# Two transformer-like layers on one core: write vectors shifted by DRAM rows, maxima turned on VectorE, work of the first layer moved between engines, and a new order

## The reference

```python
# first layer, attention place: a selective scan, then a perceptron, then a norm over (tokens, channels)
xm, res = split(xn @ in_proj_w.T);  xm = silu(causal_conv4(xm) + conv_b)
dt, B, C = split(xm @ x_proj_w.T);  delta = softplus(dt @ dt_proj_w.T + dt_proj_b)
h_t = exp(delta_t * A) * h_{t-1} + delta_t * B_t * u_t      # 512 channels x 16 states
y = (h_t . C_t + u * D) * silu(res);  m = y @ out_proj_w.T
c = m + gelu(m @ ffn_w1.T + ffn_b1) @ ffn_w2.T + ffn_b2
x = x + (c - mean(c)) / sqrt(var(c) + eps)                  # sequence 0's experts are in x too: gelu(x @ w1) @ w2, weighed
# second layer: causal softmax attention of 16 heads with 16 channels, and a memory
w1 = x_prev @ w1_write;  w2 = x @ w2_write                  # x_prev is x moved by one token, zero at token 0
write_lines = exterior(w1, w2);  read_lines = exterior(r1, r2)
mem_score = sum_j (read_i . J write_j)**2 * decay**(i - j)
out = x + (seq_out + mean(sigmoid(mem_score * s) * gate) * mem_val) @ out_w + out_b + perceptron(x)
```

## Time and profile before

| | |
|---|---|
| median of 3 runs | 3749.46 us (3745.34 to 3749.89) |
| the profiled execution | 3745.62 us, its span 3743.9 us |
| TensorE busy | 3543.0 us (95%) |
| VectorE busy | 3169.1 us (85%) |
| ScalarE busy | 2654.0 us (71%) |
| GpSimd busy | 2278.8 us (61%) |
| mean granted TensorE clock | 0.986 |

### The profile page before, as it was taken

How to read it: one execution, slowest core, us unless ns; L and a number is a source line. 1 busy time by engine, 2 the same in 40 slices (tenths; PEclk the granted TensorE clock), 3 DMA queues, 4 the chain that set the end, 5 groups by cost and what they waited for, 6 DMA issues and landing times.

```text
span 3743.9 us, 63558 instructions
## 1 busy us (share of the span) xinstructions
PE 3543.0 (95%) x20512; PEld 2364.9 (63%) x20512; DVE 3169.1 (85%) x6019; ACT 2654.0 (71%) x4087; POOL 2278.8 (61%) x1790
## 2 busy tenths in 40 slices
PE   7999999999999999999888999999999999999998
PEld 3666666656556665656665766767676676767665
DVE  3798999999999999999977688786968778696873
ACT  5878878788787878888634757566675757667565
POOL 3797999999999999999934142332514233251421
PEclk9999999999999999999898999999999999999999
DMA  4445445554554555545532123232312323231220
GB/s 155 134 162 166 161 148 181 155 170 163 167 167 148 177 166 166 170 149 178 191 97 97 42 78 101 70 109 70 115 48 81 98 70 115 64 122 48 75 84 21
DMA packets 253340, 456.88 MB, mean 122 GB/s; under 512 B 26116, under 2 KB 80852, under 8 KB 250196
## 3 DMA queue, kind: packets, MB, share of 16 engines
q1 hardware_dynamic: 253012, 452.82, 38.7%
HBM read 381.07 MB, written 69.21 MB: 120 GB/s over the span
## 4 chain that ended last, share of the span: by engine, by line
PE 50%; DVE 22%; issue 10%; ACT 8%; POOL 7%; DMA 2%; DVEq 0%; SPq 0%; POOLq 0%; ACTq 0%
DVE ps L2071 8%; PE ps L1661 6%; PE ps L1548 5%; PE ps L1653 5%; PE ps L1529 4%; POOL drive L2326 4%; PE ps L1511 3%; DVE heavy L2049 3%; ACT ps L1678 3%; PE ps L1413 3%; DVE held L2071 3%; PE ps L1463 2%; PE ps L1380 2%; ACT L1678 2%; PE ps L1588 2%
## 5 line engine op out<-in xcount | busy, mean ns | idle before, releaser
L2326 POOL TENSOR_TENSOR drive<-du,b_wide 128x1024 f32<-128x1024 f32 x512 | 1202.6, 2366 | 147.7 <-DVE held L2071 80.1
L1678 ACT ACTIVATE ps<-delta,neg_a 128x512 f32<-128x512 f32 x1024 | 684.4, 686 | 184.4 <-DVE heavy L2049 115.7
L1678 ACT ACTIVATE exps<-ps 128x1024 f32<-128x1024 f32 (+1 forms) x640 | 599.7, 939 | 228.9 <-PE ps L1529 224.9
L2360 POOL TENSOR_SCALAR_AFFINE_SELECT exps<-exps 128x256 f32<-128x256 f32 x512 | 204.4, 414 | 832.5 <-ACT exps L1678 832.5
L2094 DVE CUSTOM_DVE_ANT_0 ps<-ps,later 128x512 f32<-128x512 f32 (+3 forms) x1024 | 474.6, 518 | 55.1 <-PE ps L1511 53.1
L2049 DVE TENSOR_TENSOR heavy<-c_wide,ps 128x512 f32<-128x512 f32 x704 | 450.5, 676 | 15.2 <-issue 14.1
L1463 PEld LDWEIGHTS ps<-p_all,heavy 128*128 128x128 f32 x3072 | 355.2, 142 | 152.5 <-issue 76.9
L2071 DVE TENSOR_TENSOR_SCAN ps<-ps,carry,drive 128x512 f32<-128x512 f32 x352 | 434.8, 1274 | 10.6 <-ACT ps L1678 10.6
L1463 PE MATMUL ps<-p_all,heavy 128*128 128x128 f32 x3072 | 415.0, 277 | 23.3 <-DVE heavy L2049 20.8
L2071 DVE TENSOR_TENSOR_SCAN ps<-ps,drive 128x512 f32<-128x512 f32 x352 | 414.0, 1215 | 25.3 <-ACT ps L1678 21.9
L2310 POOL TENSOR_TENSOR held<-held,c_wide 128x1024 f32<-128x1024 f32 x160 | 378.4, 2365 | 6.4
(11 more groups left out here) (212 smaller groups left out, 7175.2 us busy)
## 6 DMA issues: line engine op xcount, KB each, us to landing
b_wide<-bc_dram SPq DMA_DIRECT2D x512, 256.0 KB, 3.4
c_wide<-bc_dram SPq DMA_DIRECT2D x512, 256.0 KB, 3.6
stacks<-parts SPq DMA_DIRECT2D x192, 256.0 KB, 2.5
qs<-stacks SPq DMA_DIRECT2D x128, 192.0 KB
ks<-stacks SPq DMA_DIRECT2D x128, 192.0 KB, 4.4
x_row<-in_x SPq DMA_DIRECT2D x14, 1024.0 KB, 7.9
resid<-mix SPq DMA_DIRECT2D x9, 1024.0 KB, 5.5
x_row<-resid SPq DMA_DIRECT2D x9, 1024.0 KB, 6.1
```

The lines of the kernel that those rows point to most:

```text
L1678: return nc.scalar.activation(out_, in_, func, **kw)
L2326: G.tensor_tensor(drive[:, g % DRIVE_SLOTS, :, :], du[:, e, :, :], wide(b_wide[:, g % B_SLOTS, :], MD), ALU.mult).then_inc(driven, 1)
```

## The change

It does the following.

- Prelude: 16 matmuls of the identity by itself before the first unit; the last four taps after the first norm, neg_a after xm; a Silu for each block of xm; Softplus on one column after the last; res units 0 and 1 moved into the order behind; the second du behind the first drive; a unit bias that transposes fb2 to late_bias.
- First layer: ScalarE drains o with a plain copy; fb2 is added in the drain of m instead, and fix (16 one-column matmuls and one subtraction) takes its product with the up weights out of fb1. gate_pair is one instruction. offset goes to GpSimd, square and shift to ScalarE.
- Second layer, memory: pb is one group of 320 columns; ScalarE drains the write vectors to ahead, and for each half SP stores them to DRAM rows one further (put) and loads them into pt1 (shift). The two memsets of a first column are gone.
- Second layer, maxima: the unit mt leaves TensorE; VectorE turns smax by four 32x32 transpositions (flip) to turned, from which mt works on ScalarE and VectorE.
- New lengths and SHIFTS for the planner, so all five lists have another order.

The diff, cut to its core:

```diff
-            + [("res", 0, t) for t in range(2)] + [("xd", 0)] + [("dl", 0, m) for m in range(MI)])
+            + [("xd", 0)] + [("dl", 0, m) for m in range(MI)] + [("bias", 0)])
...
+WARM = 16
...
                 dense(("pa", b, t), ("v", "xt", b, t // TC, KD - 1), ("v", "weights_lo", 1), ("p", "o", b - 1, NQ - 1, TQ - 1) if b else None,
                       ("v", "gate", b - 1, NC - 1) if b else None, ("p", "zt", b - 2, NC - 1, KD - 1) if b > 1 else None,
-                      a=[("g", "outer", (n - TC) // NT, (n - TC) % NT)] if n >= TC else [])
-                dense(("pb", b, t), ("p", "pa", b, t))
-                add("g", ("outer", b, t), 1.05, place["pb", b, t], ("a", "pb", b, t),
+                      a=([("g", "outer", (n - TC) // NT, (n - TC) % NT)] if n >= TC else []))
+                dense(("pb", b, t), ("p", "pa", b, t), a=[("s", "put", b - 1, NC - 1)] if b else [])
+                if t % TC == TC - 1:
+                    add("s", ("put", b, c), 0.45, place["pb", b, t], ("a", "pb", b, t), late=2.5)
+                    add("s", ("shift", b, c), 0.5, place["pb", b, t] + 1, ("s", "put", b, c),
+                        ("g", "outer", (n - TC) // NT, (n - TC) % NT) if n >= TC else None, late=2.9)
+            for t in range(TC * c, TC * (c + 1)):
+                n = NT * b + t
...
+                elif kind == "put":
+                    c = task[2]
+                    drained(sp, plan, ("pb", n, TC * c + TC - 1), "a")
+                    if (n, c) == (0, 0):
+                        sp.wait_ge(ahead_set, 1)
+                        sp.dma_start(ahead_rows[:, 0, :], none_ahead[0:B, :]).then_inc(ahead_put, 16)
+                    sp.dma_start(ahead_rows[n, 1 + c * HALF:1 + (c + 1) * HALF, :].rearrange("(t p) d -> p t d", p=P),
+                                 ahead[:, TC * c:TC * (c + 1), :]).then_inc(ahead_put, 16)
+                elif kind == "shift":
+                    c = task[2]
+                    sp.wait_ge(ahead_put, 16 * (NC * n + c + 2))
+                    if NC * n + c:
+                        sp.wait_ge(outer_done, TC * (NC * n + c))
+                    sp.dma_start(pt1[:, :, 0:64], ahead_rows[n, c * HALF:(c + 1) * HALF, :].rearrange("(t p) d -> p t d", p=P))\
+                      .then_inc(shifted, 16)
...
-                    pe.wait_ge(xm_silu, j + 1)
                     w = weight("xproj", MI)
+                    if j:
+                        pe.wait_ge(xm_silu, silus(j))
                     for m in range(MI):
+                        if j == 0:
+                            pe.wait_ge(xm_silu, m + 1)
                         last = mm(bank[0:DTR + 2 * NS, :], w[:, m, :], xm[j % 2][:, m, :], start=(m == 0),
                                   stop=(m == MI - 1))
...
+                elif kind == "bias":
+                    pe.wait_ge(params_more_in, 16)
+                    for k in range(KD):
+                        last = tp(bank[:, k * P:(k + 1) * P], param("fb2")[:, k * P:(k + 1) * P], ident)
+                elif kind == "fix":
+                    drained(pe, L0_PLAN, ("bias", 0), "a")
+                    pe.wait_ge(mlp0_up_in, 16)
+                    for m in range(MF):
+                        for k in range(KD):
+                            last = mm(bank[:, m:m + 1], w_up0[:, k, m * P:(m + 1) * P], late_bias[:, k:k + 1],
+                                      start=(k == 0), stop=(k == KD - 1))
                 elif kind == "mh":
...
             pe.wait_ge(params_in, 16)
-            pe.wait_ge(setup_a, 2)
+            for _ in range(WARM):
+                mm(ps[:, DECAY_BANKS[0], 0:P], ident, ident, start=True, stop=True)
             for unit in prelude_units():
                 if unit == ("xm", 0, 0):
                     pe.wait_ge(weights_in, 16)
+                elif unit == ("cv", 0, 0):
+                    pe.wait_ge(setup_a, 1)
                 elif unit == ("xd", 0):
                     pe.wait_ge(weights_more_in, 16)
                 side(unit)
...
                     last.then_inc(ring_filled, 1)
-                elif kind == "mt":
-                    bank = claim(plan, e)
-                    pe.wait_ge(maxed, g + 1)
-                    g %= NG
-                    tp(bank[0:2 * NT, 0:P], smax[:, 2 * g:2 * g + 2, :].rearrange("p h i -> p (h i)"), ident)\
-                        .then_inc(ring_filled, 1)
                 elif kind == "st":
                     both = claim(plan, e)
...
-                        mm(bank[:, 0:D], xT[of][:, k, tokens(t)], w[by][:, k, 0:D], start=(n == 0),
-                           stop=(n == len(three) - 1), skip_group_check=True)
-                    for n, (k, by, of) in enumerate(three):
-                        last = mm(bank[:, D:D + 64], xT[of][:, k, tokens(t, shift=0)], w[by][:, k, D:D + 64],
-                                  start=(n == 0), stop=(n == len(three) - 1), skip_group_check=True)
+                        last = mm(bank[:, 0:D + 64], xT[of][:, k, tokens(t)], w[by][:, k, :], start=(n == 0),
+                                  stop=(n == len(three) - 1))
                 elif kind == "lt":
                     c = unit[2]
...
                     f(yT[:, unit[2], :], bank, ACT.Copy).then_inc(drained_a, 1)
                 elif kind == "m":
-                    f(mT[:, unit[2], :], bank, ACT.Copy).then_inc(drained_a, 1)
+                    f(mT[:, unit[2], :], bank, ACT.Identity, bias=late_bias[:, unit[2]:unit[2] + 1]).then_inc(drained_a, 1)
+                elif kind == "bias":
+                    f(late_bias[:, :], bank[:, 0:D].rearrange("p (k n) -> p k n", k=KD)[:, :, 0], ACT.Copy).then_inc(drained_a, 1)
+                elif kind == "o":
+                    t = TC * (j % NC) + unit[2]
+                    if unit[2] == 0 and j % NC == 0:
+                        act.wait_ge(x0_stored, 16)
+                        if j:
+                            act.wait_ge(x_kept, 16 * (j // NC))
+                    f(mix[:, t, :], bank[:, 0:D], ACT.Copy).then_inc(drained_a, 1)
                 elif kind == "h":
                     m = unit[2]
+                    drained(act, L0_PLAN, ("fix", 0), "v")
                     f(h0[:, m, :], bank, ACT.Identity, bias=param("fb1")[:, m:m + 1]).then_inc(drained_a, 1)
                 elif kind == "mh":
...
+                elif kind == "square":
+                    act.wait_ge(row_apart, j + 1)
+                    f(row_q[:, 1:2], row_q[:, 4:5], ACT.Identity, scale=row_q[:, 4:5], bias=row_mv[:, 1:2]).then_inc(row_square, 1)
+                elif kind == "shift":
+                    drained(act, L0_PLAN, ("mu", j), "v")
+                    act.wait_ge(row_inverse, j + 1)
+                    f(row_q[:, 2:3], row_q[:, 0:1], ACT.Copy, scale=row_q[:, 3:4]).then_inc(row_shift, 1)
                 elif kind == "norm":
                     norm_tile(j, task[2])
                 elif kind == "centre":
                     act.wait_ge(row_shift, j + 1)
...
+            set_taps(MI - 1)
             for unit in prelude_units():
                 drain(unit)
-                if unit == ("cv", 0, MI - 1):
-                    task_of(("silu_x", 0))
+                if unit[0] == "cv":
+                    m = unit[2]
+                    drained(act, L0_PLAN, unit, "a")
+                    f(xm[0][:, m, :], xm[0][:, m, :], ACT.Silu).then_inc(xm_silu, 1)
+                    if m == MI - 1:
+                        f(late_bias[:, 0:1], eps, ACT.Softplus)
+                elif unit == ("xm", 0, MI - 1):
+                    f(neg_a[:, :], param("alog"), ACT.Exp).then_inc(setup_a, 1)
+                    act.wait_ge(setup_a, 2)
+                    f(neg_a[:, :], neg_a[:, :], ACT.Copy, scale=-1.0).then_inc(setup_a, 1)
                 elif unit == ("xt", 0, 0, KD - 1):
                     task_of(("root", 0, 1))
...
                 elif kind == "mt":
-                    bank = full(act, plan, task)
+                    act.wait_ge(flipped, n + 1)
                     if n:
                         act.wait_ge(neg_in[(n - 1) % SLOTS], 32 * ((n - 1) // SLOTS + 1))
-                    f(neg_hi, bank[0:2 * NT, 0:P], ACT.Copy, scale=-1.0).then_inc(drained_a, 1)
+                    f(neg_hi, turned[0:2 * NT, :], ACT.Copy, scale=-1.0).then_inc(neg_above, 1)
                 elif kind == "turn":
...
+                    if n == t == 0:
+                        f(none_ahead[:, :], ident[:, 0:64], ACT.Copy, scale=0.0).then_inc(ahead_set, 1)
                     f(pt1[:, t % TC, 64:128], bank[:, D:D + 64], ACT.Copy)
                     f(pt2[:, t % TC, :], bank[:, D + 64:D + 192], ACT.Copy).then_inc(drained_a, 1)
                 elif kind == "pb":
-                    f(pt1[:, task[2] % TC, 0:64], full(act, plan, task)[:, D:D + 64], ACT.Copy).then_inc(drained_a, 1)
+                    bank = full(act, plan, task)
+                    if n:
+                        act.wait_ge(ahead_put, 16 * (NC * n + 1))
```

(46 more changed lines are left out.)

153 lines of the change are left out of this document (82 added, 71 removed), and 13 rows, old and new, of the table SHIFTS.

## The result

The changed kernel takes 3752.6 us (median of 20 runs), the kernel before, on the same chip, 3745.2: ratio 1.0019, 95% interval 1.0012 to 1.0026. The forecast was 3675. Its profiled execution has a span of 3750.7 us against 3743.9. The first view of it is the one of the earlier trace rows, with the stretches moved to the new first scan and the new last gate product.

The account below looks back on a forecast made before the run. VectorE was taken to bound the first layer from 500 us, TensorE the stretch before and the second layer. Gains of 8 + 38 + 28 = 74 us gave a median of 3675 us, range 3632 to 3718.

Parts of the forecast that it names:

- the second layer's term: Second layer: 41 us of TensorE cuts, 17 or about 9 if VectorE binds crowded windows; 28 us gained was taken.
- The first layer's term: First layer from 500 us: VectorE falls by 53 us, gain between 25 and 53, taken as 38; the start adds 8.
- Start: 0 to 59.8 us: faster xm, earlier xd and drive bring the first scan 10.8 us sooner; 8 us taken.
- First layer: From 500 us: o drains, row_q and ln_shift products leave VectorE, gate products merge; three engines near level, 38 us gained.
- pb, 28 us: Second layer, TensorE: six matmuls of 320 columns save 0.44 us a tile, 28 us over 64 tiles.
- if TensorE is the bound throughout: Second layer: condition under which the pb and mt cuts on TensorE together gain their full 41 us.
- mt, 13 us: Second layer: transposition mt leaves TensorE, 8 us or 18 with its wait over 64 pairs, taken as 13.
- The queues, 0 us: Second layer: write vectors through DRAM come 8.3 us later per half, costed at nothing because other pairs' units cover it.
- The order: Second layer: sm units can be moved away from crowded windows, since VectorE has room outside; part of taking 28 us.
- Rival 2: VectorE binds the second layer's crowded windows, GpSimd or TensorE the first layer: 32 to 50 us gained, 3717 to 3699; chance 0.22.
- Its signs: Second layer: VectorE over 95% in 80 us windows, with TensorE idle on smax.
- Rival 4: Whole kernel: the order gives back what the edits gain, within 7 us of 3749; chance 0.05.

Follow-up runs that it names:

- e8: The changed kernel without the 16 matmuls ahead of the first transpositions (WARM = 0): 3747.0 us, ratio 1.0010 to the kernel before.
- e12: e5 with one more VectorE reduction ahead of each of the 64 statistics of o in the first layer: 3716.4 us, ratio 0.9937.
- e6: e5 in the same order with pb as one group of 320 columns, the shift by one token left out: 3700.9 us, ratio 0.9883.
- e9: e5's order with the edits of e6 and e7 together, no way through DRAM: 3737.8 us, ratio 0.9989.
- e10: e5 with 4.2 us less VectorE work per batch (most of the x_row bias addition and z gating left out): 3695.2 us, ratio 0.9877.
- e5: The changed kernel's first layer, the second layer's operations of before with newly searched SHIFTS: 3708.8 us, ratio 0.9904 to the kernel before.
- e7: e5 in the same order with the maxima turned by four VectorE transpositions, TensorE's transposition gone: 3739.9 us, ratio 0.9985.
- e4: The changed kernel in its own order without the detour through DRAM, write vectors unshifted: 3752.0 us, ratio 1.0022.
- e3: The changed kernel in its order, maxima turned by one 128x32 VectorE transposition instead of four, eight small transfers instead of two: 3741.4 us, ratio 0.9998.

## Why the prediction was wrong, step by step

The step that failed is the second layer's term, 28 us gained: outside 80 us of each batch it took the cuts on TensorE at their full length and the work added on VectorE at nothing. Measured are 44.8 us lost, in three parts: pb is worth 8 us alone and nothing beside flip, flip with mt costs 30, and the new order 12 to 18 more. The first layer's term was somewhat too large (38 us with the start, 46 forecast).

- **Start.** Right: xd follows cv (37.59 us, cv ends at 37.75), and the first scan comes at 50.78, 9.0 us sooner (10.8 forecast, near 49; the 8 us were taken for their worth in the whole). Wrong: the 16 matmuls don't lift xm's pace. They end at 8.33 us, TensorE then idles 3.4 us, and xm takes 10.05 us (9.62 in the earlier trace rows; 9.89 in e8).

```profile
2.94 5.39 PE L1502 MATMUL ps<-p_all 128*128 128x128 f32 x32 [2.94 <-DMA p_all<-in_params]
11.74 1.09 PE L1405 MATMUL ps<-p_all,x_row 128*128 128x128 f32 x8 [3.41 <-ACT x_row L1722]
13.96 10.05 PE L1411 MATMUL ps<-xT,w_l 128*128 128x512 f32 x16 [1.13 <-ACT xT L1722]
```

- **First layer.** 46 us forecast with the start, 38.0 measured. At the gate product of 482.49 us (497.09 before) the lead is already 14.6 us, and 23.4 come after it, where I had 38. That the three engines would stand level near 96% was right (96.0, 95.3 and 95.4% of 1364.8 us). The mis-sized term is what a VectorE cut is worth there: VectorE fell by 59 us, of which 23.4 arrived (0.40); 0.72 of a cut was taken, where e12 measured about half. ScalarE stood at 82.8% there; no row gives the 85% that the forecast set as its limit, and nothing tested it. The held row_q and ln_shift instructions went as forecast: on GpSimd offset takes 0.21 us instead of 1.48, and no row_q group left on VectorE has a mean over 0.16 us.
- **pb, 28 us.** The saving of a tile was right: the six matmuls start at 2849.78 and the next unit at 2850.76, 0.98 us (0.93 forecast). Its worth was wrong: 8 us (e6), and none beside flip (e9). This is the step "if TensorE is the bound throughout". I saw the crowding in the earlier trace rows but counted 80 us of a batch; from 2843 to 2943 us, a hundred, VectorE is at 93.31 in the kernel before, and e6 and e10 show that TensorE's 97% is no bound by itself: cuts on either engine count in part. (A slip in the forecast's sum, 75.9 for 72.3 / 0.955 = 75.7, changes nothing.)

```profile
2843.00:2943.00 100.00, 96.29 (x704) 64.79 (x707) 93.31 (x232) 64.49 (x102) 49.90 (x75) 1.00 0.39 118
```

- **mt, 13 us.** Wrong in sign, in e5's order: 30 us slower with flip (e7). The transposition that left cost TensorE 0.12 us a pair, and VectorE got 7.7 us a batch, 61 in all, where I had 35 and at most 12. flip was sized too small (0.8 us a pair for 0.55), and mt's product grew from a mean of 280 to 382 ns (399 in the changed kernel), since some are held. The Trainium skill's rule that I quoted (SBUF — State Buffer, Who interferes with whom) fits: in the changed kernel, with both inputs in SBUF, the product's median is 281 ns and its longest 878; before, with one input in PSUM, the longest is 282.
- **The queues, 0 us.** Right in the changed kernel's order (e4).
- **The order.** The forecast trusted it to move sm units out of the crowded windows. Against e5's order it costs 12 us by the ratios and 18 in the profiled executions (e9 to e4), and half clock comes with it.
- **The rivals.** Rival 2 named the right mechanism and priced it at 17 or 9 us gained in the second layer; it was 45 lost, since no term let flip and mt count outside the 80 us, or let half clock come in. Its signs came close: VectorE has 75.95 of 80 us (94.9%) from 2855 to 2935 us, and TensorE 95.3% of the stretch of 1520 us where 96 or more was to show the forecast right. That flip could cost more than all cuts on TensorE gain was in no case of mine. Rival 4, with a chance of 0.05, named the time: 3752.6 lies within 7 us of 3749. That was luck for the most part. Its reason was an order that gives back what the edits gain; the order's price is 12 to 18 us, and the larger loss is flip's.

- **Not looked for.** e5 shows what the change could have been: its first layer with the second layer of before takes 3708.8 us.

The ledger of the second layer, from the last gate to the end in the profiled executions: before 1841.1; e5, the old operations, 1842.5; e9, both edits in the old order, 1869.3; e4, the new order, 1886.8; the changed kernel, with the way through DRAM, 1885.9.

Open: what takes the half clock away in the changed kernel's order; what the computed shift costs in the old one; and what flip would cost at another place in it.

## What to carry to other kernels

Where two engines are both above 93% in a stretch, don't price a cut or an added instruction on either at its full length. In e5's order it counted for 0.4 to 0.6 of its length, in the changed kernel's order for 0.3 (e3), and pb's cut beside flip for nothing (e9); these factors are this kernel's. The share of one engine over the whole stage (80% for VectorE here) doesn't show such a stretch. An operation that is nearly free on the engine it stands on (0.12 us of TensorE for each pair) isn't worth moving to one that is nearly full. An order that was searched for one set of operations is part of them: when a change has two halves, try each half alone with its old order, as e5 did, before judging either.

## What the runs showed of the hardware that was not expected

A burst of matmuls at the start with an idle 3.4 us behind it sped only the eight transpositions after it (1.09 us, 1.94 in e8), not the xm matmuls (10.05, 9.89), which had the granted clock at 0.50 for about 6 us. Four 32x32 transpositions take 0.80 us on VectorE and one of 128x32, the same data, takes 0.207. A mean can mislead where instructions are held: the product over 128x32 has a mean of 462 ns against 399 for 16x128, but its median is 192 against 281; the means are made by a few that last up to 1268 and 878 ns. And TensorE, busy for 95% of a batch, ran some microseconds of each at half clock, right after the stretch in which it waited for VectorE.
